# Attention stage after an expert stage, one core: late keys loaded earlier, late maxima ahead of normalising, first diffusion and last value products in halves

## What is computed

```python
x = x + diffusion(x, zX, zY, zR)        # second differences along rows and columns, plus zR*y*(1-y)
x = x + experts(x)                      # 8 gated experts and a shared one: silu(x Wg) * (x Wu) @ Wd, width 512
x = x + lora(x, language) + embedding
q = (side + b_self) @ Wq + bq           # side: 16 x 128 x 128; 16 heads of 8
k = (key  + b   ) @ Wk + bk             # keys from x (masked by length) and one own key from side
w = softmax([q k_prev * scale, q k_self * scale])
x = x + (w_prev @ v_prev + w_self * v_self) @ Wo + bo
```

## Time and profile before

| what | value |
|---|---|
| runs | median 435.17 us, 434.38 to 436.15 (3) |
| profiled execution | 435.41 us, its span 433.6 us |
| TensorE busy / granted clock, mean | 417.0 us (96%) / 0.988 |
| VectorE, ScalarE, GpSimd busy | 319.2 us (74%), 271.5 us (63%), 164.4 us (38%) |
| DMA | 39.59 MB, 91 GB/s over the span |

### The profile page before, as it was taken

One profiled execution on the slowest core, in us unless ns is written; L12 is line 12 of the kernel. 1 busy time (PEld: TensorE's weight loads), 2 busy tenths in 40 slices (PEclk: granted clock), 3 DMA queues, 4 the chain that ended last, 5 costly groups with the idle time before them and its releaser, 6 DMA issues.

```text
span 433.6 us, 7156 instructions
## 1 busy us (share of the span) xinstructions
PE 417.0 (96%) x2314; PEld 326.1 (75%) x2314; DVE 319.2 (74%) x574; ACT 271.5 (63%) x517; POOL 164.4 (38%) x212
## 2 busy tenths in 40 slices
PE   8999999999999999999999999999999998999795
PEld 4676788887888877877888777778887774767473
DVE  5587777767696888776968887776698875677464
ACT  4778777765856555657565556555655558677471
POOL 1666767754322333323223333322273742121120
PEclk9999999999999999999999999999999999999798
DMA  5433353205052310000423200003864115466510
GB/s 170 137 88 103 116 162 94 76 20 167 17 158 63 121 56 9 12 17 1 145 65 108 58 20 4 26 0 116 232 187 140 48 50 164 136 178 177 156 29 26
DMA packets 53908, 39.59 MB, mean 91 GB/s; under 512 B 5132, under 2 KB 48112, under 8 KB 53648
## 3 DMA queue, kind: packets, MB, share of 16 engines
q1 hardware_dynamic: 53440, 39.04, 30.8%
q10 hardware_dynamic: 432, 0.10, 0.1%
HBM read 27.29 MB, written 11.90 MB: 90 GB/s over the span
## 4 chain that ended last, share of the span: by engine, by line
PE 82%; DVE 9%; ACT 4%; issue 3%; DMA 1%; SPq 1%; DVEq 0%; ACTq 0%
PE acc_ps L573 7%; PE acc_ps L569 7%; PE acc_ps L570 7%; PE g_ps L573 7%; PE g_ps L569 7%; PE g_ps L570 7%; PE u_ps L573 7%; PE u_ps L569 7%; PE u_ps L570 7%; PE st_ps L715 3%; PE s_ps L634 2%; PE g_ps L678 2%; PE tp_ps L735 2%; DVE neg_key L1072 2%; PE pv_ps L726 2%
## 5 line engine op out<-in xcount | busy, mean ns | idle before, releaser
L836 ACT ACTIVATE act_hi<-u_ps 128x512 fp32r<-128x512 f32 x144 | 86.1, 598 | 90.2 <-DVE u_ps L1083 78.0
L1087 DVE TENSOR_TENSOR act_lo<-u_ps,act_hi 128x512 fp32r<-128x512 f32 x144 | 99.2, 689 | 49.4 <-ACT act_hi L836 45.3
L1083 DVE TENSOR_TENSOR u_ps<-act_p,u_ps 128x512 f32<-128x512 f32 x144 | 99.8, 693 | 26.2 <-ACT act_p L831 22.5
L831 ACT ACTIVATE act_p<-g_ps 128x512 f32<-128x512 f32 x144 | 85.8, 596 | 29.5 <-PE g_ps L573 28.3
L1252 POOL TENSOR_TENSOR xg_lo<-xg,xg_hi 128x512 fp32r<-128x512 f32 x35 | 45.6, 1304 | 134.8 <-ACT xg_hi L842 134.8
L569 PE MATMUL acc_ps<-act_hi,w_split 128*128 128x512 f32 x144 | 59.3, 412 | 0.0
L569 PE MATMUL u_ps<-xg_hi,w_split 128*128 128x512 f32 x144 | 57.3, 398 | 0.2 <-ACT xg_hi L842 0.2
L573 PE MATMUL acc_ps<-act_lo,w_split 128*128 128x512 f32 x144 | 57.0, 396 | 0.3 <-DVE act_lo L1087 0.2
L569 PE MATMUL g_ps<-x_hi,w_split 128*128 128x512 f32 x144 | 56.4, 391 | 0.7 <-ACT x_hi L885 0.7
L573 PE MATMUL u_ps<-xg_lo,w_split 128*128 128x512 f32 x144 | 56.6, 393 | 0.0
L570 PE MATMUL acc_ps<-act_hi,w_split 128*128 128x512 f32 x144 | 56.5, 392 | 0.0
(11 more groups left out here) (155 smaller groups left out, 640.0 us busy)
## 6 DMA issues: line engine op xcount, KB each, us to landing
k_blk<-k_rows SPq DMA_DIRECT2D x64, 64.0 KB, 2.3
q_blocks<-q_rows SPq DMA_DIRECT2D x32, 128.0 KB, 2.6
q_pl<-q_rows SPq DMA_DIRECT2D x16, 192.0 KB, 2.8
k_plain<-k_rows SPq DMA_DIRECT2D x8, 384.0 KB, 3.9
w_raw<-in_L_cond_Wg SPq DMA_DIRECT2D x8, 256.0 KB, 2.7
w_raw<-in_L_cond_Wu SPq DMA_DIRECT2D x8, 256.0 KB, 2.7
w_raw<-in_L_cond_Wd SPq DMA_DIRECT2D x8, 256.0 KB, 2.8
q_rows<-rows_hi SPq DMA_DIRECT2D x8, 256.0 KB, 2.9
```

The source lines that it names most:

```text
L831: activation(act_p[m % 2][:], g_ps[m % 2][:], ACT.Silu).then_inc(silu_done, 1)
L836: activation(act_hi[m % 3][:], u_ps[m % 3][:], ACT.Identity).then_inc(act_hi_done, 1)
L1083: tt(u_ps[m % 3][:], act_p[m % 2][:], u_ps[m % 3][:], ALU.mult).then_inc(prod_done, 1)
L1087: tt(act_lo[m % 3][:], u_ps[m % 3][:], act_hi[m % 3][:].bitcast(F32), ALU.subtract).then_inc(act_lo_done, 1)
```

## The change

- SP: `load_keys(15)` is issued right behind `load_keys(14)`, ahead of pair 6; `store_out(4, 6)` goes ahead of the placement of batch 12; the last two batches are stored one by one.
- LATE_FINISH: each step but key half a block later.
- TensorE: the second late scores of a block go ahead of turn_pv. VectorE: both maxima of a block go ahead of normalise and make_out.
- Start: x in two loads, all steps of the first diffusion in two halves, the second half in another bank than the first (s_ps, aux_ps).
- End: the value products of batch 15 go half into pv_ps, half into st_ps[1], and are copied out in two pieces; normalise(15) goes ahead of make_out(14); three and four products without use are put in (`keep_warm`).
- ScalarE: a one-element Exp behind the last silu; exp_self of batches 0 to 11 behind the first four exponentials.

```diff
+HALVES = slice(0, TB // 2), slice(TB // 2, TB)
-LATE_FINISH = {(0, 0): "lora_a", (0, 1): "lora_b", (1, 1): "key", (2, 0): "value", (2, 1): "x_natural"}
+LATE_FINISH = {(0, 1): "lora_a", (1, 0): "lora_b", (1, 1): "key", (2, 1): "value", (3, 0): "x_natural"}
...
+            def load_first(n):
+                half = HALVES[n]
+                sp.dma_start(x_in[:, half], blockwise(a["x"][half])).then_inc(first_loaded[n], 16)
...
-            load_x(0)
+            for n in range(2):
+                load_first(n)
...
             load_keys(done + 2)
+            load_keys(done + 3)
             load_pair(6)
+            store_out(4, 6)
             place_max(done)
-            store_out(2)
-            load_keys(done + 3)
             load_pair(7)
             place_max(done + 1)
-            store_out(3)
+            store_out(6, 8)
             place_max(done + 2)
-            store_out(4)
+            store_out(8, 10)
             place_max(done + 3)
...
+            store_out(14, 15)
+            store_out(15, 16)
...
-            diffuse(0)
+            for n, (half, bank, written) in enumerate(zip(HALVES, (s_ps, aux_ps), (first_written, aux_written))):
+                pe.wait_ge(first_ready, n + 1)
+                pe.wait_ge(y_ready, n + 1)
+                for b in range(half.start, half.stop):
+                    to = bank[:, (b - half.start) * S:(b - half.start + 1) * S]
+                    mm(to, dif_a[:, b], ident, start=True, stop=False)
+                    last = mm(to, x_y[:, b], lap_t, start=False, stop=True)
+                last.then_inc(written, 1)
...
                 for i in range(GI):
                     pe.wait_ge(exp_done, b * GI + i + 1)
+                    bank, at = (pv_ps, i) if b < B - 1 or i < GI // 2 else (st_ps[1], i - GI // 2)
...
             for b in range(B):
-                late_work(b, 0)
+                late_finish(b, 0)
+                late_scores(b, 0)
+                late_turn(b)
                 if b >= 2:
                     turn_attn(b - 2)
                 if b + 1 < B:
                     for i in range(GI):
                         scores_t((b + 1) * GI + i)
+                late_scores(b, 1)
                 if b >= 1:
                     turn_pv(b - 1)
...
-                late_work(b, 1)
+                late_finish(b, 1)
...
             turn_attn(B - 2)
+            keep_warm(3)
             turn_pv(B - 1)
             project(B - 2)
+            keep_warm(4)
             turn_attn(B - 1)
...
+                    if t == NT - 1 and k == SLOTS - 1:
+                        activation(warm[:, 1:2], warm[:, 0:1], ACT.Exp)
...
-            exp_self(0, B - TB)
             for i in range(GI):
                 exp_scores(i)
+            exp_self(0, B - TB)
...
+            def take_last():
+
+                half = GI // 2
+                dve.wait_ge(pv_written, B * GI - half)
+                wait(dve, pv_turned, B - 1)
+                nc.vector.tensor_copy(pv_own[:, 0:half].rearrange("p i s -> p (i s)"), pv_ps[:, 0:half * S])
+                dve.wait_ge(pv_written, B * GI)
+                nc.vector.tensor_copy(pv_own[:, half:].rearrange("p i s -> p (i s)"), st_ps[1][:, 0:half * S]).then_inc(pv_taken, 1)
...
                 if b >= 1:
                     take(b - 1)
-                late_work(b, 0)
+                late_finish(b, 0)
+                late_maxima(b, 0)
+                late_maxima(b, 1)
                 if b >= 1:
                     normalise(b - 1)
                 if b >= 2:
                     make_out(b - 2)
-                late_work(b, 1)
-            take(B - 1)
+                late_finish(b, 1)
+            take_last()
+            normalise(B - 1)
             make_out(B - 2)
-            normalise(B - 1)
             make_out(B - 1)
```

More of the change, by code:

```diff
@@ L266, in build @@
         first_split = sem("first_split")
+        first_loaded = [sem(f"first_loaded{n}") for n in range(2)]
+        first_step, first_ready, first_written = sem("first_step"), sem("first_ready"), sem("first_written")
         z_ready, x_scaled, x_padded, x_weighted = sem("z_ready"), sem("x_scaled"), sem("x_padded"), sem("x_weighted")
@@ L744, in project, with keep_warm, late_finish, late_scores @@
                 mm(tp_ps[b % 2][:, D:2 * D], attn_t[:], w_raw4[:, 3], start=True, stop=True).then_inc(out_written, 1)
-            def late_work(b, place):
+            def keep_warm(products):
+                for _ in range(products):
+                    mm(st_ps[0][:, 0:D], w_raw4[:, 3], w_raw4[:, 3], start=True, stop=True)
+            def late_finish(b, place):
                 if (b, place) in LATE_FINISH:
                     aux_step(LATE_FINISH[b, place], NT - 1, 0)
+            def late_scores(b, place):
                 if (b, place) in LATE_SCORES:
                     scores(*LATE_SCORES[b, place], aux_ps)
-                if place == 0 and b in LATE_TURN:
+            def late_turn(b):
+                if b in LATE_TURN:
                     pe.wait_ge(attn_done, b - 1)
@@ L1099, in _ @@
             tt(z_own[:], z_own[:], z_all[:, 2], ALU.add).then_inc(z_ready, 1)
-            dve.wait_ge(x_loaded, 16)
             dve.wait_ge(z_ready, 2)
[L1102 to L1106, removed]
+            for n, half in enumerate(HALVES):
+                dve.wait_ge(first_loaded[n], 16)
+                for b in range(half.start, half.stop):
+                    ts(dif_b[:, b], x_in[:, b], z_less[:, b:b + 1], z_own[:, b:b + 1], ALU.mult, ALU.add).then_inc(x_weighted, 1)
+                dve.wait_ge(x_weighted, half.stop)
+                tt(dif_b[:, half], dif_b[:, half], x_in[:, half], ALU.mult).then_inc(first_step, 1)
+                dve.wait_ge(x_padded, n + 1)
+                tt(dif_a[:, half], x_x[:, half, 0:D], x_x[:, half, 2:D + 2], ALU.add).then_inc(first_step, 1)
+                dve.wait_ge(first_step, 2 * n + 2)
+                tt(dif_a[:, half], dif_a[:, half], dif_b[:, half], ALU.add).then_inc(first_ready, 1)
             dve.wait_ge(gate_loaded, 32)
@@ L1115, in _ @@
             dve.wait_ge(aux_rounded, 1)
-            tt(x1_lo[0][:], aux_ps[:], x1_hi[0][:].bitcast(F32), ALU.subtract).then_inc(first_split, 1)
+            for half, bank in zip(HALVES, (s_ps, aux_ps)):
+                some = slice(half.start * S, half.stop * S)
+                tt(x1_lo[0][:, some], bank[:, 0:N // 2], x1_hi[0][:, some].bitcast(F32), ALU.subtract).then_inc(first_split, 1)
             dve.wait_ge(gates_ready, 2)
-            tt(xg[:], aux_ps[:].rearrange("p (b s) -> p b s", b=TB), over_s(gates[:, 0, 0:TB]), ALU.mult).then_inc(xg_made, 1)
+            for half, bank in zip(HALVES, (s_ps, aux_ps)):
+                last = tt(xg[:, half], bank[:, 0:N // 2].rearrange("p (b s) -> p b s", s=S),
+                   gates[:, 0, half].unsqueeze(2).to_broadcast([128, TB // 2, S]), ALU.mult)
+            last.then_inc(xg_made, 1)
             dve.wait_ge(xg_rounded, 1)
@@ L1205, in late_work, with late_maxima @@
                         nc.vector.tensor_copy(warm[:, 0:1], v_all[:, B - 1, H - 1, DH:VW]).then_inc(v_direct, 1)
+            def late_maxima(b, place):
                 if (b, place) in LATE_SCORES:
```

71 lines of the change are left out of this document (42 added, 29 removed).

## The result

The changed kernel takes 429.65 us (429.11 to 430.68, 4 runs) against 435.5 us (434.38 to 436.15, 4 runs) for the kernel before: ratio 0.9889, 95% interval [0.985, 0.9929] (the two medians alone give 0.9866). The forecast was 429.2 us, faster. A repeat of the changed kernel gave 428.99 us, ratio 0.988 [0.9854, 0.9906]. In the profiled executions the span fell from 433.6 to 427.2 us, the mean granted clock rose from 0.988 to 0.999.

The account below looks back on a forecast made before the run. TensorE, 96% busy, was taken as the bound, losing most at late keys of batch 15 behind SP's queue. 5.05 + 1.0 + 0 = 6.05 us off 435.41 gave 429.4, as median 429.2 us; range 426.8 to 432.8 us.

Parts of the forecast that it names:

- The stall at 404 us: TensorE's 2.50 us hole waiting for late keys of batch 15 goes, and the half clock after it; gain 5.05 us.
- The three new waits: TensorE waits 0.75 to 0.85 us each for the placements of batches 12, 13 and 14, replacing the big one.
- rival 1: SP does not bind, pair 6 and placements land sooner, blocks 11 to 13 run free: 427.1 us, chance 0.13.
- The SP queue after 376 us: First key load moves from 376.09 to 376.0 us, then SP issues without pause; block 4 ends 0.15 us earlier.
- Blocks 5 to 12: Attention stage: VectorE's cycle bounds at 3.5 us per block against 3.79, but waiting for batch 14's keys keeps nearly nothing.
- The table load at 0: Exp load of 1.28 us on ScalarE moves behind the last silu; TensorE's 0.15 us loss hides in the key wait.
- The end: Last 7 us: earlier normalise 0.45 us, last projection at full clock 0.4 us, other small parts; sum 1.0 us.
- The start at 0: First diffusion in halves still begins at 9.30 us; taken as 0, gain at most 0.2, loss at most 0.3 us.
- The clock: Assumption that TensorE's granted clock holds at 1.00 to the end, over the three waits for placements.
- rival 2: Clock falls once in the waits of blocks 8 or 11 to 13, costing 3.0 us: 432.2 us, chance 0.15.
- The starting point: The 6.05 us come off the profiled execution of 435.41 us, giving 429.4; the median lies 0.24 us below it.
- the 3.05 us for half clock: TensorE's loss from 6.1 us at half speed after the hole ahead of 406.54 us, where it is the bound.

Follow-up runs that it names:

- Keys 15 back: Changed kernel with the keys of batch 15 loaded again behind pair 6 and the placement of batch 12: 431.77 us, ratio 0.9949.
- the SP order alone: Kernel before with only the keys of batch 15 issued ahead of pair 6 and the third store ahead of the first placement: 432.37 us, ratio 0.9961.
- the last variant of the SP queue: Changed kernel with pair 6 between keys 14 and 15, first stores behind placement 12, placement 13 ahead of pair 7, no warm products: 426.94 us, ratio 0.9826.

## Why the prediction was right, point by point

- **The stall at 404 us**: right in cause and place. Keys 15 back brings it and the half clock back.
- **The three new waits**: forecast 0.85 at batch 12, 0.75 at 13 and 0.85 at 14; measured 0.77, 1.29 and none. The placement of 13 took 3.07 us to land and not 2.33, and the wait for it left time for that of 14. The last term was 416.05 us for the products of batch 15, measured 415.81. Two slips of the sum are small: a plain block was put at 2.9 us from the 415.30 of the earlier trace rows, which is where the chain enters products that start at 415.06, and measured 3.04 (412.77 to 415.81); and the three waits add up to 2.45 us, where rival 1 gives back 2.05.
- **The SP queue after 376 us**: the step that failed. "That becomes 376.0" was 374.50. 0.30 us came from the expert stage and 0.20 from the rounding of the key rows (0.1 forecast). The other 1.09 us is the landing of the key rows' low part: 4.41 us before, 3.32 after. In the four kernels with the old places of the finishing steps it took 4.4 to 4.6 us, in the ten others 3.1 to 3.3, so it belongs to the change and not to chance. Start, table load, late maxima and warm products were put back one by one and left it short; no run moved the finishing steps alone. I had taken it as fixed. Block 4 therefore did not wait for the keys of batch 12, and the take of block 9 came at 396.46, not 397.6. The error hardly reached the end, in part by luck. The lead was 0.8 us at pair 6 (issued from 395.80, forecast 396.6) and 0.6 us at the placement of 12 (waited for until 404.95, forecast 405.55); the slow landing of the placement of 13 (until 409.84, forecast 409.45) ate the rest.
- **Blocks 5 to 12**: 3.57 us from take to take (381.30, 384.87, 388.45, 392.01); forecast 3.5.
- **The table load at 0**: right for the sum of the moves, wrong as a reading of the part. With the load and exp_self, which move together, 1.16 us are gained on the way to the key rows and 1.5 to 2.3 us in all, yet before and after differ by only 0.20 us there: the rest of the change, it seems the finishing steps half a block later, gives the other part back. That was not tried alone. The Trainium skill (ScalarE: Activation LUTs, What ACT_TABLE_LOAD costs) gives some 1.28 us for the load, which the trace has to the digit, and a drain that makes it 2.66 us, which it doesn't show: the load at 358.04 us is followed by the next activation at 359.33, in the changed kernel too.
- **The end**: 0.83 us from the products of batch 15 to the last make_out (10.26 to 9.43), and 0.27 behind it (2.23 to 1.96, a smaller last store): 1.1 for 1.0. The clock holds without the warm products, so that part of the sum has no effect to show.
- **The start at 0**: right, tried alone.
- **The clock**: held in the changed kernel's profiles, as assumed, but not in all its executions. Two of the four behind the 429.65 us had a mean clock of 0.996 and took 430.04 and 430.68 us; none of the four of the repeat did. So rival 2 came about in two of eight, at 0.8 to 1.5 us over the forecast and not at 3.0. The variants with the old start and the old table load, and the SP order alone, show the same.
- **The starting point**: the 6.05 us were taken off an execution in which the mean clock (0.988) was almost the lowest seen (0.987). The kernel before kept it in 12 of 65 later ones, which took 431.95 us, and its medians there were 434.1 to 434.6 us. Had one of those been profiled, the 3.05 us for half clock would have had nothing to stand on.

Sum in the profiled executions: 0.30 from the expert stage, 63.36 - 58.36 = 5.00 to batch 15, 1.10 at the end: 6.4 us, the difference of the spans (forecast 6.05). The medians differ by 5.3 us (repeat) and 5.85 us (first result).

## What to carry to other kernels

When DMAs are issued in one hand-written order, add up that queue like an engine: a load wanted soon must not stand behind an issue that waits for a landing, and a small placement can go ahead of a large load (one profile shows it, the medians do not yet). Taking away a wait upstream is worth only what the queue lets through. Before costing a moved step at zero, test its part alone: two moves that cancel look like two moves that do nothing. And look at the granted clock of many executions before pricing what a fall of it costs: one profile shows a fall or none.

## What was not expected of the hardware

- The granted clock fell after much less idle time than in the old hole: after 1.81 us in one piece, and after 0.74, 0.36 and 1.00 us within 6 us. It stayed at 1.00 over 1.29 us with 0.77 us five microseconds ahead, and over 1.33 us with 0.49 us as far ahead. The same program kept it in some executions and not in others (2 of 4 and 4 of 4 for the changed kernel).
- One issue of a key or query load on SP takes 0.60 to 0.64 us as a rule, but four of them took 2.5 to 4.2 us in different executions, with no cause that the profile shows.
- The store of the key rows' low part landed in 3.1 to 3.3 or 4.4 to 4.6 us, the long ones in the four kernels with the old places of the finishing steps. What ties the two together was not found.
- The end of the expert stage varies by 1.7 us (last silu 356.58 to 358.26), and the start explains most of it: the first silu came at 13.87 us in the former and at 15.26 in the latter. The first rows below are the changed kernel (first silu at 14.72), the second the last variant of the SP queue (13.87). The warm-up products take 0.86 us less there. Their weight loads show why: they are 0.34 us long and come every 0.85 us at first, then 0.19 us long and every 0.43 us, half of both, and the step lies at 6.70 us in the one and at 4.99 us in the other. That is what the half level of the clock would do, though the profile shows the granted clock as 1.00 from the start in both. What sets the moment is open.

```profile
1.49 7.96 PE L688 MATMUL g_ps<-act_p 128*128 128x512 f32 x12 [1.49 <-DVE act_p L1143]
...
5.91 0.34 PEld L688 LDWEIGHTS g_ps<-act_p 128*128 128x128 f32 x1 [0.52 <-issue]
6.70 0.19 PEld L688 LDWEIGHTS g_ps<-act_p 128*128 128x128 f32 x1 [0.45 <-issue]
```

```profile
1.48 7.10 PE L688 MATMUL g_ps<-act_p 128*128 128x512 f32 x12 [1.48 <-DVE act_p L1141]
...
4.21 0.34 PEld L688 LDWEIGHTS g_ps<-act_p 128*128 128x128 f32 x1 [0.52 <-issue]
4.99 0.19 PEld L688 LDWEIGHTS g_ps<-act_p 128*128 128x128 f32 x1 [0.45 <-issue]
```
